# Four-layer graph network on one core: which queue issues the node-row copy, and the order of the first gathers

## The reference, cut to what matters

```
x = layernorm(x + attention(x, edges, edge_attr_8))      # softmax over the edges of one target
x = layernorm(x + messages(x, edges, edge_type_16))      # relu message, mean over a target's edges
x = layernorm(x + equivariant(node_vec1, edges, ...))
x = layernorm(x + hypergraph(hypergraph(x)))             # two convolutions, batch norm between
```

## Time and profile before

| what | us |
|---|---|
| median of 3 runs (lowest, highest) | 2453.09 (2450.83, 2456.04) |
| the profiled execution's own time | 2452.97 |
| its span in the trace | 2451.1 |
| VectorE busy | 1576.9 (64%) |
| GpSimd busy | 1650.2 (67%) |
| TensorE matmuls busy | 1380.3 (56%) |
| index phase | about 12 to 291.6 |
| attention phase | 291.6 to 682.9 |

### The profile page before, as it was taken

One profiled execution on the slowest core, in us unless ns is written; L12 is line 12 of the kernel. 1 busy time (PEld: TensorE's weight loads), 2 busy tenths in 40 slices (PEclk: granted clock), 3 DMA queues, 4 the chain that ended last, 5 costly groups with the idle time before them and its releaser, 6 DMA issues. The chain is left out here.

```text
span 2451.1 us, 21738 instructions
## 1 busy us (share of the span) xinstructions
PE 1380.3 (56%) x4580; PEld 717.5 (29%) x4580; DVE 1576.9 (64%) x4895; ACT 861.6 (35%) x1813; POOL 1650.2 (67%) x1319
## 2 busy tenths in 40 slices
PE   5378668888748787467878366254566630011111
PEld 1134334444423333223334234122333420001110
DVE  8379749899839999849998444233355573524443
ACT  0011027777637777726768212011113320000000
POOL 0277288787168867066674588787877877878877
PEclk9689879999868998778989689677788865555555
DMA  7611225444266666254655677567898863323331
GB/s 243 219 31 35 59 69 125 117 119 124 64 145 166 168 178 167 76 112 110 149 135 135 128 203 200 127 184 191 138 253 240 228 168 76 86 58 71 73 72 43
DMA packets 355456, 324.17 MB, mean 132 GB/s; under 512 B 107805, under 2 KB 309292, under 8 KB 354845
## 3 DMA queue, kind: packets, MB, share of 16 engines
q1 hardware_dynamic: 260925, 251.63, 37.4%
q0 software_dynamic: 94400, 71.15, 15.0%
HBM read 226.10 MB, written 122.90 MB: 142 GB/s over the span
## 5 line engine op out<-in xcount | busy, mean ns | idle before, releaser
L2221 DVE TENSOR_TENSOR_SCAN tl_S<-tl_same,tl_S,tl_pX 128x500 f32<-128x500 bf16 x96 | 120.4, 1254 | 298.7 <-issue 172.9
L2105 PE MATMUL tl_pX<-k_ident,tl_ga 125*128 125x125 f32 x400 | 85.3, 352 | 388.4 <-DMA tl_ga<-table_TE,k_s_idxE 309.3
L477 POOL DMA_INDIRECT tl_ga<-table_TE,k_s_idxE x200 | 244.4, 1222 | 63.5 <-issue 58.6
L284 POOL DMA_INDIRECT table_XW<-k_ef,ix_scatI x100 | 120.8, 1208 | 120.8 <-issue 120.8
L477 POOL DMA_INDIRECT ms_ga<-table_T,k_idxS x100 | 145.4, 1454 | 56.6 <-issue 28.1
L2105 PEld LDWEIGHTS tl_pX<-k_ident,tl_ga 125*128 125x128 f32 x400 | 58.9, 180 | 403.7 <-DMA tl_ga<-table_TE,k_s_idxE 319.3
L477 POOL DMA_INDIRECT eq_ga<-table_T,k_idxS x100 | 127.4, 1274 | 65.8 <-ACT eq_y L1789 37.6
L1300 DVE TENSOR_TENSOR dr_o<-dr_x,tl_pMul 128x512 f32<-128x512 f32 x98 | 67.0, 684 | 135.3 <-PE tl_pMul L1284 91.5
L1283 PE MATMUL tl_pCon<-dr_BC,dn_cT 128*128 128x512 f32 x196 | 132.5, 764 | 38.3 <-ACT dn_cT L1290 33.4
L477 POOL DMA_INDIRECT at_ga<-table_XW,k_src x100 | 126.4, 1264 | 40.5 <-issue 29.6
L477 POOL DMA_INDIRECT at_gb<-xw,at_dstI x100 | 129.8, 1298 | 30.5 <-issue 30.5
(11 more groups left out here) (462 smaller groups left out, 4314.2 us busy)
## 6 DMA issues: line engine op xcount, KB each, us to landing
table_XW<-xw SPq DMA_DIRECT2D x5, 5156.2 KB, 50.8
dr_x<-x SPq DMA_DIRECT2D x97, 256.0 KB
result<-dr_o SPq DMA_DIRECT2D x97, 256.0 KB
dm_xT<-xT SPq DMA_DIRECT2D x32, 768.0 KB
tl_fac<-table_dinv SPq DMA_DIRECT2D x50, 250.0 KB
table_T<-at_y SPq DMA_DIRECT2D x50, 224.0 KB
table_T<-ms_y SPq DMA_DIRECT2D x50, 224.0 KB
table_T<-eq_y SPq DMA_DIRECT2D x50, 224.0 KB
```

What stands on the lines that cost most here:

```text
L284: nc.gpsimd.indirect_dma_start(out=T["XW"], out_offset=bass.IndirectOffsetOnAxis(ap=scatI[:, t:t + 1], axis=0), in_=K["ef"][:, t:t + 1], i ...
L477: nc.gpsimd.indirect_dma_start(out=buf[:, k, :], out_offset=None, in_=table, in_offset=bass.IndirectOffsetOnAxis(ap=index[:, CT * c + k:CT ...
L2105: last = nc.tensor.transpose(pX[j % 2][:, k * TP:(k + 1) * TP], ga[j % RG][:, k, :], K["ident"][0:TP, 0:TP])
L2221: nc.vector.tensor_tensor_scan(S[i][:], same[j % RM][:], pX[i][:, 0:CE], 0.0 if j % NC == 0 else S[1 - i][:, CE - 1:CE], ALU.mult, ALU.add ...
```

## The change

Four edits:

1. The five pieces of the copy are issued by ScalarE at the start of its index phase, behind a wait for all 13 small loads, and no longer by SP. `prior` and the source blocks then follow the 13 loads directly in SP's queue. The view of the table is written with 2000 rows instead of 400.
2. In attention, dstI is loaded first, with a semaphore of its own; GpSimd waits for it alone.
3. `fetch` gathers target rows (and does the s_z wait) before source rows.
4. In the message phase GpSimd does not wait for the seven weights any more.

```diff
@@ index_phase, sync
-            for i in range(PIECES):
-                n = N // PIECES
-                sp.dma_start(T["XW"][n * i * DW:n * (i + 1) * DW, :].rearrange("(a b) o -> a (b o)", a=400),
-                             g["xw"][n * i:n * (i + 1), :].rearrange("(a b) c -> a (b c)", a=400)).then_inc(s_tab, 16)
@@ index_phase, scalar
+            act.wait_ge(s_in, 16 * 13)
+            for i in range(PIECES):
+                n = N // PIECES
+                act.dma_start(T["XW"][n * i * DW:n * (i + 1) * DW, :].rearrange("(a b) o -> a (b o)", a=2000),
+                              g["xw"][n * i:n * (i + 1), :].rearrange("(a b) c -> a (b c)", a=2000)).then_inc(s_tab, 16)
@@ attention_phase
-        DONE = 16 * 8
+        DONE = 16 * 7
+        s_targets = a.sem("targets")
@@ attention_phase, sync
+            sp.dma_start(dstI[:], g["dst_col"]).then_inc(s_targets, 16)
             for n in W:
                 sp.dma_start(W[n][:], g[n]).then_inc(s_w, 16)
...
             sp.wait_ge(s_init, 2)
-            sp.dma_start(dstI[:], g["dst_col"]).then_inc(s_w, 16)
@@ attention_phase, gpsimd
-            pool.wait_ge(s_w, DONE)
             nc.gpsimd.memset(eps[:], EPS).then_inc(s_eps, 1)
+            pool.wait_ge(s_targets, 16)
 
             def fetch(c):
+                need(pool, s_z, c - RB + 1)
+                gathers(pool, s_gb[c % RB], dstI, c, g["xw"], gb[c % RB])
                 need(pool, s_tA, c - RA + 1)
                 need(pool, s_z2, c - RA + 1)
                 gathers(pool, s_ga[c % RA], K["src"], c, T["XW"].rearrange("(n c) o -> n (c o)", c=DW), ga[c % RA])
-                need(pool, s_z, c - RB + 1)
-                gathers(pool, s_gb[c % RB], dstI, c, g["xw"], gb[c % RB])
@@ message_phase, gpsimd
             nc.gpsimd.memset(eps[:], EPS).then_inc(s_eps, 1)
-            pool.wait_ge(s_w, 16 * 7)
```

## The result

The changed kernel takes 2431.62 us (median of 7 runs, 2426.74 to 2440.61) against 2454.65 for the kernel before on the same chip (2449.52 to 2456.04). The ratio is 0.9914, 95% interval 0.9897 to 0.9932: 21 us faster, between 17 and 25 (the two medians lie 23 us apart). The profiled execution took 2431.6, its span 2429.8 (2451.1 before).

A forecast was written before the change was run, and what follows sets the result against it. Three phase starts where everybody waits for a DMA were taken as the limit, with compute setting attention's later pace. Index 10 + attention 10 + message 5 = 25 us, from 2452.97 to 2428; own range 2421 to 2435, whole 2404 to 2441.

The forecast's parts named there:

- Part 1: Index phase, copy issued by ScalarE: one or two rounds run ahead, the next waits for the copy; 10 us gained.
- the blocks pass the copy: Index phase: small loads pass the copy, VectorE never waits, the scatter ends the phase; gain 30.4 us, total 2408; chance 0.28.
- Part 2: Attention's start: dstI loaded first comes 3.05 us earlier, and all gathers with it.
- Part 3: Attention's start, targets gathered first: targets 9.1 us, sources 6.7, chunk 3 9 to 11 earlier; 10 taken, Part 2 included.
- the prediction's own sign of being wrong: Attention: the forecast is wrong if TensorE waits for `at_gb` or `at_ga` after chunk 4.
- The slack of 6 us: Attention's steady state: source rows land 6 us or so before their turn, which hides the target gather's wait for the residual.
- the refill wait: Attention, slower rival: target gathers wait for the residual and hold source gathers; 34 us over 20 chunks, 2462; chance 0.04.
- Part 4: Message phase's start: gathers begin 6.19 us earlier without the wait for weights; 5 us gained, bounds 0 and 8.
- the whole one: The full range of the forecast total, from below the first rival (2404) to the second one's end (2441).

The follow-up runs named there:

- the copy alone: The kernel before with only the copy's issue moved from SP to ScalarE; ratio 0.9956 (0.9942 to 0.9969).
- the even blocks: Changed kernel with first five source blocks in one load, loads split 112 + 13 rows, dsame and dpen stores behind three blocks; ratio 0.9848 (0.9825 to 0.9871).
- sources first: Changed kernel with attention's gather order put back, source rows ahead of target rows; ratio 0.9930 (0.9917 to 0.9943).
- seven buffers: Changed kernel with seven buffers for target rows instead of five; ratio 0.9931 (0.9917 to 0.9945).

## Why the prediction was right, and where it wasn't

The total was right: 2428 forecast, 2431.62 measured. Its terms were not all, and that they came out near it together is partly luck.

- **Part 1, 10 us.** The size was right: 11.4 in the two profiles, 8.7 on average over the five traces with this index phase (attention from 280.25, 284.98, 282.33, 282.17 and 284.81, mean 282.9, against 291.64), 10.8 (8 to 14) in the time of the copy alone. The course was right too: two rounds ahead, then the wait to 107. The reason was half right. "A small transfer waits for pieces of the other queue" is what the counts show; but I let block 2 wait for the copy, and it was the two stores ahead of it on SP's queue, on 10 engines, and then its own 25 turns on 5. The copy and scatter moved by 4.6 us, not 1.4, since the copy is issued 1.6 us later and its last DMA lands 83.3 us after its issue instead of 80.3, probably because it now shares its engines with small loads (no run tests that alone).
- **Rival, the blocks pass the copy (28%).** It did not happen, and the even blocks show what it lacked: blocks that are through before the copy fills the engines. With it the phase ended at 266.90, where the rival had put 261.2.
- **Part 2, 3 us.** Right. With the gathers' order as before, c17 stands at 248.9 with dstI first and at 252.3 without (three traces, 252.0 to 252.6): 3.4.
- **Part 3, the step that failed.** The chunks up to 4 gained what I said or nearly (target turn of chunk 0 7.6 instead of 9.1, sources 7.3 instead of 6.7, chunk 4 9.9 in 9 to 11). But I took 10 for the phase from chunk 3, and did not ask whether the gathers could feed the chunks behind it. They begin only 3.8 us earlier against the phase's start (2.39 instead of 6.16), need 12.2 to 13 us a chunk, and so the compute that had gained 9.9 had used up their reserve by chunk 5, where a landing of 6.7 us (I had reckoned with 2.2) made it wait: 3.1 us lost there, 2.1 behind it at a granted clock of 0.77. That is the prediction's own sign of being wrong, a wait for `at_ga` after chunk 4. At c17 the seven traces with targets first and five buffers have a mean of 248.0, 0.8 below the one trace of sources first: of Part 3's 6 us at chunk 4, at most about 1 is left. The phase gained 3.2 us on average (392.2 in three traces with the old order and constants, 388.95 in seven with the new), not 10.
- **The slack of 6 us.** TensorE's waits for source rows did come, but not through the refill wait: with it gone chunk 5 waited 2.65 us all the same.
- **Part 4, 5 us.** Right on average (4.2), 7.0 in the profile.

The errors cancelled in part: against the forecast the profile has +1.4, -8 and +2, and 0.8 from later phases. By the means 8.7 + 3.2 + 4.2 = 16.1, just under the measured 17 to 25, and near the 17 that sources first and seven buffers give on another chip. That would be 2437, outside the 2421 to 2435 that the forecast gave as its own range and inside the whole one.

Still open: chunk 18 of attention takes 16.5 us in the changed kernel instead of the 13.6 before, with a granted clock of 0.86 from 528 to 552 against 1.00 before, that is partly at 1.2 instead of 2.4 GHz (0.86 to 0.93 in four of the other traces, 1.00 in sources first). The kernel before and sources first have such a chunk too, only earlier: chunk 10 at a granted clock of 0.89, 15.3 us instead of 13.6. It costs 1.4 to 3 us where it comes; what decides when it comes, no run here tells.

## What to carry to other kernels

When a start is brought forward, compare the head start of the consumer with that of its supplier: what the first chunks gain beyond the supplier's own shift comes out of the supply's reserve, and is lost at the first chunk where that is gone, here with one late landing. Work that the supplier can do ahead, in time in which it is idle, keeps its gain (14 us here, for eight gathers). For a load that must pass a long transfer, count turns: rows divided by the engines that carry them, one for each piece of the other queue, and all that stands ahead of it on its own queue; 112 + 13 rows need 8 turns where 125 need 25. Better still is to have the load through before the long transfer fills the engines, as the first load of the even blocks was.

## What the runs showed of the hardware that was not expected

- SP's and ScalarE's queues take turns packet by packet on an engine, whatever the sizes: 210 packets of SP's queue to 196 pieces of 26,400 bytes in 20 us. A 250-byte row cost a whole piece of the copy.
- The number of rows decides the engines: the copy with 100 pieces a DMA ran at 271 GB/s and with 1,000 at 243, each at 63 to 65% of 16 engines (10 in 16 are 63%), with 96 at 321 and 96%. The shorter pieces may have their part in the 243.
- Issuing can hang far off the data's own engine: ScalarE stood 95 us in the issue of ten DMAs of 1,000 pieces, 33 us with 100 pieces each, SP 46.66 us in one store.
- A wait of TensorE can cost more than itself: in the eight traces where chunk 5 waited 2.3 to 3.1 us, chunk 6 took 13.1 to 15.7 us, 14.7 or more in seven of them; in the six where it did not, 12.7 (granted clock 0.77 against 1.00 in the two shown). That the wait brings the lower clock is read from this pattern; no run tests it alone.
- The same code's phases differ from execution to execution: the message phase without its wait took 358.7 to 370.0 us in ten traces. A difference of 5 us between two profiles of a phase says little by itself.
